# A graph and attention layer with routed experts: the stores of x1 moved behind the block loop, and the expert weights loaded from ScalarE's queue

## The reference

```
xn = layernorm(x)
x1 = x + gnn(xn, src, dst) + mix(xn) @ Wo        # mix: linear attention with random features
out = x1 + moe(layernorm(x1))

gnn: for each edge e with destination d:  msg_e = V[src_e] * softmax over the edges of d of a leaky logit
     rst[d] = sum of msg_e                       # 8 heads of 64
moe: gates = layernorm(x1) @ gate_w (512x8); 8 rounds of Sinkhorn scaling;
     each of the 8 experts takes its 6250 // 8 = 781 best tokens, y = (x512) @ experts[e] (512x512);
     rows with a gate <= 0.5 give 0; the sum is divided by (1 + how many experts took the token)
```

## Time and profile before

| | us |
|---|---|
| median of 3 runs | 3434.51 |
| the profiled execution | 3419.7 |
| its span in the trace | 3417.9 |
| block stage, first to last gather | 1687 to 2998 |
| the last addition of x1 (block 49) | 3019.5 to 3020.2 |
| DVE begins the one-hot matrices behind its wait for the stores | 3153.9 |
| first gather of rows for the experts | 3184.6 |

### The profile page before, as it was taken

One profiled execution on the slowest core, in us unless ns is written; L12 is line 12 of the kernel. 1 busy time (PEld: TensorE's weight loads), 2 busy tenths in 40 slices (PEclk: granted clock), 3 DMA queues, 4 the chain that ended last, 5 costly groups with the idle time before them and its releaser, 6 DMA issues.

```text
span 3417.9 us, 46952 instructions
## 1 busy us (share of the span) xinstructions
PE 2742.1 (80%) x10591; PEld 1696.2 (50%) x10592; DVE 1549.3 (45%) x2425; ACT 991.3 (29%) x2549; POOL 2276.2 (67%) x1845
## 2 busy tenths in 40 slices
PE   4659999999999788831377778888999999943998
PEld 2346667676767544511233444454555555532543
DVE  5612222222222377726733444555555565656432
ACT  2312222222222100002144444454555555520111
POOL 7277777877777777760288888787777777700354
PEclk9879999999999999976699999898999999965999
DMA  5421111111111233351155566667677777740111
GB/s 151 134 69 33 27 36 27 30 27 36 27 30 27 62 90 89 89 77 17 48 160 158 160 161 171 175 173 177 174 182 182 184 189 183 184 136 0 36 48 41
DMA packets 285719, 342.03 MB, mean 100 GB/s; under 512 B 167601, under 2 KB 186776, under 8 KB 285416
## 3 DMA queue, kind: packets, MB, share of 16 engines
q0 software_dynamic: 218592, 223.91, 28.9%
q1 hardware_dynamic: 64515, 113.60, 11.1%
q10 hardware_dynamic: 2562, 3.97, 0.4%
HBM read 286.72 MB, written 55.05 MB: 100 GB/s over the span
## 4 chain that ended last, share of the span: by engine, by line
POOL 37%; PE 22%; issue 19%; DVE 10%; DMA 6%; DVEq 3%; ACTq 1%; ACT 1%; SPq 1%; POOLq 0%
POOL R L504 29%; PE ps L586 20%; POOL R L538 7%; DMA R<-val_tab,src_i 3%; POOL er_starts L516 2%; DVE R L1288 1%; DMA R<-el_tab,src_i 1%; DVEq L1291 1%; DVEq L1288 1%; DMA work<-in_x_dram 1%; PE ps L847 1%; DVE work L1379 1%; DVEq L1292 1%; DVE R L1324 1%; DVE R L1268 0%
## 5 line engine op out<-in xcount | busy, mean ns | idle before, releaser
L586 PE MATMUL ps<-R,work 125*125 (+3 forms) x5240 | 1795.2, 492 | 122.8 <-DVE R L1288 96.4
L586 PEld LDWEIGHTS ps<-R,work 125*125 125x125 f32 (+2 forms) x5240 | 878.2, 194 | 961.2 <-issue 954.2
L538 POOL DMA_INDIRECT R<-val_tab,src_i x800 | 1050.0, 1313 | 423.0 <-issue 192.9
L504 POOL DMA_INDIRECT R<-el_tab,src_i x800 | 981.4, 1227 | 362.1 <-issue 362.1
L1288 DVE TENSOR_TENSOR R<-R (+1 forms) x800 | 515.8, 689 | 577.7 <-POOLq L544 305.3
L988 ACT ACTIVATE work<-work 125x125 f32<-125x125 f32 x900 | 277.6, 308 | 555.9 <-PE ps L586 462.8
L586 PE MATMUL ps<-work,R 128*128 128x250 f32 x1600 | 359.5, 383 | 49.8 <-DVE work L1150 49.8
L985 ACT ACTIVATE work<-work,negdst 125x125 f32<-125x125 f32 x900 | 353.4, 393 | 112.1 <-issue 87.5
L586 PEld LDWEIGHTS ps<-work,R 128*128 128x128 f32 x1600 | 309.0, 194 | 87.1 <-issue 49.9
L586 PE MATMUL ps<-R 128*128 (+5 forms) x716 | 171.2, 390 | 70.6 <-DVE work L1202 39.5
L1160 DVE TENSOR_TENSOR R<-ps,R 125x512 f32<-125x512 f32 x50 | 34.6, 691 | 356.9 <-PE ps L586 356.9
(11 more groups left out here) (234 smaller groups left out, 2075.9 us busy)
## 6 DMA issues: line engine op xcount, KB each, us to landing
R<-el_tab,src_i POOLq DMA_INDIRECT x800
R<-val_tab,src_i POOLq DMA_INDIRECT x800
work<-in_x_dram SPq DMA_DIRECT2D x25, 500.0 KB
work<-R SPq DMA_DIRECT2D x25, 500.0 KB
val_tab<-R SPq DMA_DIRECT2D x50, 250.0 KB
work<-in_x_dram SPq DMA_DIRECT2D x50, 250.0 KB
xm_tab<-work SPq DMA_DIRECT2D x50, 250.0 KB
work<-xm_tab SPq DMA_DIRECT2D x50, 250.0 KB
```

The lines of the kernel that those rows point to most:

```text
L504: eng.indirect_dma_start(out=ELP[:, t % CT, t // CT, :], out_offset=None, in_=el_tab[:, :], in_offset=bass.IndirectOffsetOnAxis(ap=src_i[: ...
L538: eng.indirect_dma_start(out=ring[:, (2 * u + s) % RING, :], out_offset=None, in_=val_tab[:, :], in_offset=bass.IndirectOffsetOnAxis(ap=sr ...
L586: return pe.matmul(o, l, r, start=start, stop=stop)
```

## The change

Two things are moved, and nothing is added or left out. On SP the block loop is split in two: first all 50 loads of x + mix, with the same conditions as before, then all 50 stores of x1, with the same conditions as before. And the eight loads of the experts' weights, with the two waits ahead of them, stand in ACT's program behind its last work for the blocks.

```diff
             for t in range(4):
                 load_xm(t)
+            with eng.Fori(4, T) as t:
+                hold(S["x1_ready"], t - 3)
+                load_xm(t)
+
+
             for t in range(3):
                 store_x1(t)
             with eng.Fori(4, T) as t:
-                hold(S["x1_ready"], t - 3)
-                load_xm(t)
                 store_x1(t - 1)
             store_x1(T - 1)
-
-            eng.wait_ge(S["block_summed"], T)
-            eng.wait_ge(S["acc_free"], T + 2)
-            for e_ in range(X):
-                eng.dma_start(exp_w[:, e_, :, :], experts[e_].rearrange(wv4, p=128)).then_inc(S["experts_loaded"], 16)
...
             staggered(act, ((0, lambda c: copy_sums(c, block_onehots(c))), (2, deviation2), (4, last_xn2)))
+
+            act.wait_ge(S["block_summed"], T)
+            act.wait_ge(S["acc_free"], T + 2)
+            for e_ in range(X):
+                act.dma_start(exp_w[:, e_, :, :], experts[e_].rearrange(wv4, p=128)).then_inc(S["experts_loaded"], 16)
```

## The result

The changed kernel is slower, by less than forecast. In its first timing the medians are 3453.0 us against 3428.4 us, a ratio of 1.0069, 95% interval 1.0047 to 1.0091. A second timing of the same two kernels, with six and 17 runs, gave 3458.3 against 3423.9, 1.0105 (1.0083 to 1.0128). So the cost is 25 to 34 us, where 48 was forecast.

The account below looks back on a forecast made before the run. The chain is mostly POOL and PE; after the blocks, DVE's wait for the 50th store moves the end. + 55 - 7 = + 48 on 3419.7 gives 3468, or 3482 on the medians' scale; range 3448 to 3529.

Parts of the forecast that it names:

- The first store goes when block 45 is done, not behind the last block: On SP: the last load goes at about 2972, when block 45 is done, and the first store at 2973.2.
- Rival 4's lower neighbour: On SP: stores begin only behind the last block, 3020.5 + 215 + 8 = 3244, 90 us late; 7% together with rival 4.
- A trip of 4.3 us in quiet: SP's stores: each waits until the one before has landed, 4.3 us a trip, bounds 3.85 to 5.0.
- Rival 1: At DVE's wait: stores are short trips of 2.1 to 2.6 us, hidden by the routing; not slower, 3427; 7%.
- the hint on few DMA engines: Store trip: 1.45 us plus 2.5 of transfer over five engines is 3.95, from the DMA share of 0.18.
- Four stores until 3003, and 8 us lost to the experts' weights: SP's row: four stores beside the last gathers; collision with the experts' weights on the DMA engines loses 8 us (2 to 15).
- DVE idle some 55 us: At DVE's wait for the 50 stores: one-hot matrices start at 3209 instead of 3153.9, 55 us later; bounds 28 to 94.
- The experts' loads on ACT cost nothing: On ACT: weights land at 3055 instead of 3045, 135 us ahead of PE's first product, costing nothing.
- The tail unchanged, 264 us: Beyond DVE's wait: POOL and PE unchanged, 264 us to the end.
- The block stage gains 7 us (0 to 15): Block stage: half of POOL's 17.8 us waiting for gathers, less 2 for the last two blocks, comes back: 7 us.
- rival 2: Block stage: short hidden trips, and stores delayed gathers each block; all 17.8 (POOL) + 16.0 (PE) us back, 3401; 3%.
- The low end of the range, 3448: Whole kernel: 28 us late at DVE's wait less 15 back in the block stage is 13, 3448.

## Why the prediction was wrong, point by point

The direction was right, and so was the mechanism of the delay: the stores form a row of round trips, the row outlasts the routing, DVE waits for it, and the end moves with DVE. Measured by the steps:

- *The first store goes when block 45 is done, not behind the last block.* Right: 1.2 us after that x1. Rival 4's lower neighbour is out.
- *A trip of 4.3 us in quiet.* 4.2, within the bounds 3.85 to 5.0. The loads of the same tile, 4.35, were the right row to lean on. Rival 1, 2.1 to 2.6 us, is out; the two terms of the hint on few DMA engines, 1.45 and 2.5, are 2.2 and 2.0 by the run with five in flight. By the rule of the Trainium skill on how many engines a DMA uses (DMA: Bandwidth & Descriptors, "Why a DMA increments its semaphore by 16 and not by 1") 125 partitions go over 5 of the 16 and 120 over 15; the share of 0.33 and the shorter trip of the cut store agree with that, and no view lists the engines.
- *Four stores until 3003, and 8 us lost to the experts' weights.* Four in 30 us are 7.5 us a trip beside gathers; it was 7.0, over five trips. The experts cost some 12 us of the row, by the run that moves them. The 4 us more there and the 4 us less by trips of 4.2 for 4.3 cancel: the row was 238 us from the first store to DVE's start (2944.0 to 3182.5), forecast 236. That the two terms of contention came out so near is luck: no row had a trip beside other traffic, and for the first anything from two and a half to seven stores was open.
- *DVE idle some 55 us.* 54.5 and 54.6.
- *The experts' loads on ACT cost nothing.* Right by their own run, 1.0001.
- *The tail unchanged, 264 us.* Right.
- *The block stage gains 7 us (0 to 15).* **This is the step that failed.** Two pairs of profiles show 1069.3 and 1072.1 before, 1054.1 and 1050.8 after: 15 to 21 us, 18 in the middle, and the timings some 25. I took the 17.8 us under gathers in the earlier trace rows, halved them, and wrote that the 39.2 us that POOL waits for PE "are no part of it, since PE itself is nearly full". They were the main part. A store and the load behind it, in flight together, cost POOL these waits; parting them takes the waits away. How that comes about is argued, not followed in a trace: sharing few DMA engines they delay a bundle of gathers, DVE and PE get their tiles late and all at once and give the ring's slots back late, and POOL meets that as a wait for PE. This collision is what rival 2 named, at 3%; it was priced there with all of the 17.8 and the 16.0, and tied to short trips, so no case had both the long row and the large gain. Most of the 17.8, 12 of it, were the 0.3 us gaps of 40 gathers; of the 39.2, 22 were gaps and 17 real. The real waits of before were 26.1 us in all (25.0 in the second profile), after none. I had the row that shows it, the longest wait of 2.6 us against a gap of 0.3, and read only its total.

With 18 for 7 the sum is 55 - 18 = 37, so 3471 on the scale of the medians shown then and 3465 on the 3428.4 of the first timing. The timings give 25 and 34, a little less. Part of this is that the two profiled executions of the kernel before, both of 3419 to 3420 us, were short ones; its medians are 3424 to 3434. By the medians of one group, the changed kernel with cut stores, which has the gain and no pause, is 25 us below the kernel before, and the changed kernel is 59 above that one. So the sum in a middling execution is nearer 55 - 25 = 30, an estimate that lies between the two timings. Why these two, of the same kernels, differ by 9 us isn't shown.

The low end of the range, 3448, allowed 15 us of gain only together with the shortest trips; the time of 3453 is inside the range. The size of the forecast is what missed, 48 for 25.

The kernel that the runs point to is the one before with one wait more, or with its stores cut at 120 rows: 3398.7 and 3400.2 us, ratios 0.9927 and 0.9903. Moving the stores away gained the same in the block stage and paid 55 us for it at the end.

## What to carry to other kernels

A transfer that waits for the one before costs a whole round trip; it is free only where something else sets the pace, so price a moved row of them as count by trip, from any row of lone transfers of the same shape. In the view of waits, subtract the engine's fixed gap (here 0.3 us) from every group before judging it, look at the longest wait, and ask whose lateness a wait for a busy engine really is: in a ring, late input may come back as a late release. Profile the same kernel twice and set both executions beside the median before a term is taken from one. Two transfers in flight together can cost what neither costs alone; parting them in time, or spreading their rows, is a small edit to try before anything is moved.

## What the runs showed of the hardware

- A tile of 125x512 float32 (256 KB) from SP takes 4.2 us to DRAM in quiet when lone, from issue to the next issue behind its landing. With five in flight there is one each 2.0 us, at a DMA share of 0.33 and 127 GB/s. Cut into 120 and 5 rows it takes 2.8 us with both parts awaited and both issues.
- The same store takes 7.0 us beside the last gathers (184 GB/s on all engines from 2944 to 2979), and 8.8 beside eight loads of 1 MB each (330 GB/s from 3008 to 3035).
- Adding a second 256 KB store to each of 50 blocks cost nothing (ratio 0.9969), while parting the existing store from the load behind it by one wait gained 27 us (0.9927).
